# B's diagonal images by DMA, dt matmuls in pairs on two row tiles, and a new job order for a scan kernel on four engines

## The reference

```
xi, z = split(h_normed @ in_proj);  xi = silu(causal_conv4(xi))
dt, Bm, Cm = split(xi @ x_proj)                 # 16, 16, 16 columns
dt  = softplus(dt @ dt_proj + dt_bias)          # 512 channels
dA  = exp(dt[..., None] * A);  dBu = dt[..., None] * Bm * xi[..., None]
h_t = dA_t * h_(t-1) + dBu_t                    # scan over time, 512 channels x 16 states
y   = sum_s(h * Cm) + xi * D;  out = (y * silu(z)) @ out_proj;  h += out
```

## Time and profile before

| | |
|---|---|
| time, median of 3 runs | 8187.27 us (8179.34 to 8187.66) |
| time of the profiled execution | 8192.45 us |
| its span, first to last instruction | 8190.5 us |
| PE busy | 7500.0 us (92%) |
| PEld busy | 5200.0 us (63%) |
| DVE busy | 6520.6 us (80%) |
| ACT busy | 5866.5 us (72%) |
| POOL busy | 6376.4 us (78%) |
| mean granted clock of TensorE | 0.978 of full |

### The profile page before, as it was taken

How to read it: one execution, slowest core, us unless ns; L and a number is a source line. 1 busy time by engine, 2 the same in 40 slices (tenths; PEclk the granted TensorE clock), 3 DMA queues, 4 the chain that set the end, 5 groups by cost and what they waited for, 6 DMA issues and landing times. The chain is left out here.

```text
span 8190.5 us, 204523 instructions
## 1 busy us (share of the span) xinstructions
PE 7500.0 (92%) x86656; PEld 5200.0 (63%) x86656; DVE 6520.6 (80%) x6490; ACT 5866.5 (72%) x10937; POOL 6376.4 (78%) x3556
## 2 busy tenths in 40 slices
PE   7888799999989899999988899999988899999989
PEld 4666466666664566666664666666664666666655
DVE  4888799999984499999983599999973699999972
ACT  5776687878774578787764678877764687778753
POOL 5886399999991499999980599999980699999970
PEclk8998899999999999999999999999999999999999
DMA  1111111111110111111110111111110111111110
GB/s 60 52 53 60 43 52 50 64 46 50 46 48 27 43 63 49 50 46 50 52 42 27 58 50 46 50 46 60 56 38 21 54 50 46 50 59 57 46 39 11
DMA packets 133325, 391.29 MB, mean 48 GB/s; under 512 B 49580, under 2 KB 78188, under 8 KB 95552
## 3 DMA queue, kind: packets, MB, share of 16 engines
q1 hardware_dynamic: 132416, 378.22, 13.1%
HBM read 364.93 MB, written 13.24 MB: 46 GB/s over the span
## 5 line engine op out<-in xcount | busy, mean ns | idle before, releaser
L1220 DVE TENSOR_TENSOR_SCAN arena<-arena,ps 128x512 f32<-128x512 f32 x4608 | 5341.5, 1205 | 606.1 <-issue 380.3
L1445 POOL TENSOR_TENSOR arena<-arena 128x1024 f32<-128x1024 f32 x2240 | 5250.6, 2365 | 428.7 <-DVE arena L1220 399.6
L563 PEld LDWEIGHTS ps<-arena 64*128 64x128 f32 x36864 | 2334.3, 190 | 1338.3 <-issue 750.5
L897 ACT ACTIVATE arena<-arena,rate 128x511 f32<-128x511 f32 (+1 forms) x4608 | 3036.3, 710 | 43.3 <-DVE arena L1220 43.0
L563 PE MATMUL ps<-arena 64*128 64x128 f32 x36864 | 2759.6, 286 | 266.9 <-DVE arena L1220 260.9
L582 PE MATMUL ps<-csts,arena 64*128 64x64 f32 x35840 | 1516.1, 223 | 27.8 <-POOL arena L1445 27.8
L582 PEld LDWEIGHTS ps<-csts,arena 64*128 64x128 f32 x35840 | 1432.3, 140 | 40.7 <-POOL arena L1445 33.7
L621 PE MATMUL ps<-arena 128*128 128x512 f32 x1152 | 633.3, 650 | 144.8 <-DVE arena L1250 137.8
L1454 POOL TENSOR_TENSOR arena<-csts,arena 128x512 f32<-128x512 f32 x576 | 603.1, 1049 | 81.1 <-ACT arena L1022 81.1
L894 ACT ACTIVATE arena<-arena 128x2 f32<-128x2 f32 x2048 | 405.4, 198 | 326.7 <-DVE arena L1220 319.5
L661 PE MATMUL ps<-arena 128*128 128x512 f32 x1120 | 604.1, 636 | 15.6 <-DVE arena L1255 7.7
(11 more groups left out here) (118 smaller groups left out, 7014.6 us busy)
## 6 DMA issues: line engine op xcount, KB each, us to landing
arena<-c_rows SPq DMA_DIRECT2D x288, 1024.0 KB, 4.8
arena<-ip_x SPq DMA_DIRECT2D x20, 512.0 KB, 4.4
arena<-ip_z SPq DMA_DIRECT2D x20, 512.0 KB, 4.1
arena<-op_w SPq DMA_DIRECT2D x20, 512.0 KB, 3.8
hT<-xT SPq DMA_DIRECT2D x16, 512.0 KB, 3.7
arena<-w SPq DMA_DIRECT2D x8, 1024.0 KB, 5.2
out<-arena SPq DMA_DIRECT2D x64, 128.0 KB, 1.7
arena<-xp_w SPq DMA_DIRECT2D x20, 160.0 KB, 2.5
```

Source lines behind the costliest of these rows:

```text
L563: i = nc.tensor.matmul(o, dtxT[half[h], c, b, :], diagB[half[h], pair, b, :].rearrange("p (i s) -> p i s", s=Q), start=True, stop=True)
L897: nc.scalar.activation(o, i, ACT.Exp, scale=rate[:, ph.layer(n), g:g + 1]).then_inc(decay.sem, 1)
L1220: nc.vector.tensor_tensor_scan(hs[:, place(n, v) + g % 2, :], dA[:, g % RING, :], pair[:, g % Q::Q], 1.0 if ph.main() else 0.0, ALU.mult, ...
L1445: nc.gpsimd.tensor_tensor(hs[:, a:a + 2, :], hs[:, a:a + 2, :], Crep[:, 2 * pair:2 * pair + 2, :], ALU.mult).then_inc(prod.sem, 1)
```

## The change

1. POOL's `diag` is gone. SP keeps two images of the full `diagB` layout in DRAM (`b_image`, 2 MB each, zeroed once at the start). In each step it writes B's values onto the diagonals with two DMAs of 64 partitions (each 2,048 runs of 8 bytes), waits until they have landed, and then loads the eight parts of `diagB` (256 KB each, in runs of 512 bytes), each when PE has made the last input that reads the old part. PE waits on these loads (`diag_loaded`). The order of B's and C's loads on SP is written out in `LOADS`.
2. `xp` gives 97 rows: dt and the one stand a second time behind B, in rows 80 to 96. `dt0` and `dt2` multiply rows 0 to 32, `dt1` and `dt3` rows 64 to 96 (B's rows there meet zeros in the weights), in two banks, next to each other in PE's table. `bT` transposes only rows 64 to 96.
3. `rstd` no longer loads its table in main steps from the third of a block on.
4. The tables of PE, ACT, DVE and POOL and the banks are new, for main and prefix steps. SP's `body` is split into `fetch`, `replace` and `after`; in main steps the load of `op_w` comes after the loads of B and C.

```diff
-XP = 80
+XP = 97
+DT_ROWS = DR + DS + 1
...
-MAIN_PE = {0: [("z1.1", 1)], 2: [("z2.0", 1), ("z2.1", 1)], 3: [("z3.0", 1)], 4: [("z3.1", 1)], 5: [("yt2", -1)],
-           6: [("yt3", -1), ("xp.0", 1)], 7: [("xp.1", 1), ("xp.2", 1)], 8: [("xp.3", 1), ("dxT3", 0)], 9: [("bT", 1)],
-           10: [("dt2", 1)], 11: [("dt3", 1), ("ms", 2)], 12: [("dt0", 1)], 13: [("dt1", 1)],
-           15: [("out0.0", -1), ("out0.1", -1)], 16: [("out0.2", -1)], 17: [("out0.3", -1)], 18: [("xi0.0", 2)],
-           19: [("xi0.1", 2), ("yt0", 0)], 20: [("dxT0", 1)], 21: [("xi1.0", 2)], 22: [("xi1.1", 2)], 23: [("yt1", 0)],
-           24: [("xi2.0", 2)], 25: [("xi2.1", 2), ("dxT1", 1)], 26: [("out1.0", -1)],
+MAIN_PE = {0: [("z1.1", 1), ("z2.0", 1)], 2: [("z3.0", 1), ("z2.1", 1)], 3: [("z3.1", 1)], 5: [("yt2", -1)],
+           6: [("xp.0", 1), ("xp.1", 1), ("yt3", -1)], 7: [("xp.2", 1), ("xp.3", 1)], 8: [("dxT3", 0)], 9: [("bT", 1)],
+           10: [("dt2", 1), ("dt3", 1)], 12: [("dt0", 1), ("dt1", 1)], 14: [("ms", 2)],
+           15: [("out0.0", -1), ("out0.1", -1), ("out0.2", -1)], 16: [("out0.3", -1)], 18: [("xi0.0", 2)],
+           19: [("xi0.1", 2), ("yt0", 0)], 20: [("dxT0", 1)], 21: [("xi1.0", 2), ("xi1.1", 2)], 22: [("yt1", 0)],
+           24: [("xi2.0", 2), ("xi2.1", 2)], 25: [("dxT1", 1)], 26: [("out1.0", -1)],
...
-            12: [("dt0", 1), ("skip3", 0)], 13: [("dt1", 1), ("rstd", 2)], 14: [("soft", 1), ("carry", 1)], 19: [("xi0", 2)],
+            12: [("dt0", 1), ("dt1", 1), ("skip3", 0)], 13: [("rstd", 2)], 14: [("soft", 1), ("carry", 1)],
...
-PRE_ACT_FIRST = {2: [("yev3", -1)], 10: [("yev0", 0)], 19: [("yev1", 0)], 28: [("yev2", 0)]}
+PRE_ACT_FIRST = {3: [("yev3", -1)], 10: [("yev0", 0)], 19: [("yev1", 0)], 26: [("yev2", 0)]}
...
+LOADS = [("B", 0), ("B", 1), ("B", 2), ("B", 3), ("C", 0), ("B", 4), ("B", 5), ("C", 1), ("B", 6), ("B", 7), ("C", 2),
+         ("C", 3)]
...
-                    pe.wait_ge(diag_ready.sem, diag_ready.at(ph, n, pair + 1))
+                    pe.wait_ge(diag_loaded[pair], ph.count(1, n, 1) * 16)
...
-                    i = nc.tensor.matmul(o, dtw[0:DR + DS + 1, c * P:(c + 1) * P], xdbl[0:DR + DS + 1, :],
-                                         start=True, stop=True)
+                    rows = slice(B_ROW, XP) if c % 2 else slice(0, DT_ROWS)
+                    i = nc.tensor.matmul(o, dtw[rows, c * P:(c + 1) * P], xdbl[rows, :], start=True, stop=True)
...
-                    nc.scalar.preload_act_table_set(LOG_EXP)
+                    if not ph.main() or m < 2:
+                        nc.scalar.preload_act_table_set(LOG_EXP)
...
-            def diag(ph, m, pair):
...
+                    for h in range(2):
+                        sp.dma_start(diagonal(m % 2, h), xbc[half[h], m % 2, :, :].rearrange("p b (q s) -> p (b q) s", s=Q)
+                                     ).then_inc(b_stored, 16)
+
+            def replace(ph, n):
+                m = n + 1
+                if m < ph.steps:
+                    sp.wait_ge(b_stored, ph.count(1, m, 1) * 32)
+                    sp.sem_inc(passed, 1)
+                    for what, k in LOADS:
+                        if what == "B":
+                            sp.wait_ge(input_ready.sem, input_ready.at(ph, n, PAIRS - CQ + k + 1))
+                            sp.dma_start(diagB[:, k, :, :], image(m % 2)[k]).then_inc(diag_loaded[k], 16)
+                        else:
+                            sp.wait_ge(prod.sem, prod.at(ph, n, UNITS - CU + 2 * k + 2))
+                            sp.dma_start(Crep[:, 4 * k:4 * k + 4, :],
+                                         c_rows[m % 2, 4 * k:4 * k + 4, :].partition_broadcast(P)).then_inc(c_loaded[k], 16)
```

More of the change, by code:

```diff
@@ L27 @@
 NB = T // P
+IMAGE = P * NB * CQ * P
 RING = 8
@@ L43 @@
 PRE_BANK = {"out0": 1, "yt3": 0, "out1": 0, "dxT1": 0, "ms": 1, "dxT2": 0, "xi0": 0, "xi1": 1, "dxT3": 0, "xi2": 0,
[L44 to L47, removed]
+            "xi3": 1, "z0": 0, "z1": 0, "z2": 1, "z3": 1, "yt0": 0, "xp": 1, "yt1": 1, "bT": 1, "dt2": 1, "dt3": 0,
@@ L48 @@
+            "dt0": 1, "dt1": 1, "yt2": 1, "dxT0": 0}
+MAIN_BANK = {"z0": 0, "z1": 1, "z2": 0, "z3": 1, "yt2": 0, "yt3": 1, "xp": 0, "dxT3": 1, "bT": 1, "ms": 1, "dt0": 0,
+             "dt1": 1, "dt2": 0, "dt3": 1, "out0": 0, "xi0": 1, "yt0": 0, "dxT0": 0, "xi1": 1, "yt1": 0, "xi2": 1,
              "dxT1": 0, "out1": 0, "xi3": 1, "dxT2": 1}
 PARTS = {"ms": KD, "xi": KD, "z": KD, "xp": KI, "out": KI}
-PRE_PE = {1: [("dxT1", 0), ("out0.1", -1)], 2: [("out0.2", -1)], 3: [("yt3", -1)], 5: [("out0.3", -1), ("out1.0", -1)],
[5 rows of a table removed]
@@ L203, in program @@
 def program(nc, xT, ctxT, w_early, ip_x, ip_z, xp_w, dt_w, op_w, a_log, d_par, pre_w1, pre_w2, cst,
-            cst_attention, avec, wq, wk, wv, wp, w1, w2, b2, kept, c_rows, out):
+            cst_attention, avec, wq, wk, wv, wp, w1, w2, b2, kept, c_rows, b_image, out):
     ctx = ExitStack()
@@ L634, in job @@
                     await_read_of(pe, ph, m, "xp")
+                    rows = slice(B_ROW, XP)
                     for b in range(NB):
-                        i = nc.tensor.matmul(o[:, b * XP:(b + 1) * XP], xdbl[0:XP, b::NB], eye[0:XP, 0:XP],
+                        i = nc.tensor.matmul(o[:, b * DT_ROWS:(b + 1) * DT_ROWS], xdbl[rows, b::NB], eye[rows, rows],
                                              start=b == 0, stop=b == NB - 1, is_transpose=True)
@@ L1486, in body @@
                         event(ph, m, name)
-                    if v >= UNITS - CU and ph.has(n, 1):
-                        diag(ph, n + 1, v - (UNITS - CU))
             def attend(ph, then):
@@ L1518, in rows, with image, diagonal @@
                 return v.rearrange("(k p) m -> p k m", p=P)
+            def image(par):
+                return b_image[par * IMAGE:(par + 1) * IMAGE].rearrange("(p b q c) -> q p b c", p=P, b=NB, q=CQ)
+            def diagonal(par, h):
+                row = IMAGE // P
+                a = par * IMAGE + h * 64 * row
+                rows_of = b_image[a:a + 64 * (row + Q)].rearrange("(i x) -> i x", i=64)
+                return rows_of[:, 0:row].rearrange("i (g c) -> i g c", c=P)[:, :, 0:Q]
             for dst, src in ((csts[:, :], cst), (avecs[:, :], avec), (rate[:, :, :], a_log), (Dall[:, :, :], d_par)):
@@ L1522, in _, with next_out, fetch @@
             sp.wait_ge(cst_ready, 1)
+            def next_out(ph, n):
+                if 1 <= n < ph.steps and ph.slot(n - 1) == ph.slots - 1:
+                    await_done(sp, ph, n - 1, "out1")
+                    sp.dma_start(opw, rows(op_w[ph.layer(n)])).then_inc(opw_loaded, 16)
             def body(ph, n):
+                fetch(ph, n)
+                if n + 1 >= 0:
+                    replace(ph, n)
+                    after(ph, n)
+            def fetch(ph, n):
                 m = n + 1
@@ L1548, in body @@
                                  ).then_inc(init_loaded, 16)
-                if 1 <= n < ph.steps and ph.slot(n - 1) == last:
-                    await_done(sp, ph, n - 1, "out1")
-                    sp.dma_start(opw, rows(op_w[ph.layer(n)])).then_inc(opw_loaded, 16)
+                if not ph.main():
+                    next_out(ph, n)
                 if m < ph.steps:
@@ L1570, in body, with after @@
                     sp.sem_inc(passed, 1)
-                    for k in range(4):
-                        sp.wait_ge(prod.sem, prod.at(ph, n, UNITS - CU + 2 * k + 2))
-                        sp.dma_start(Crep[:, 4 * k:4 * k + 4, :], c_rows[m % 2, 4 * k:4 * k + 4, :].partition_broadcast(P)
-                                     ).then_inc(c_loaded[k], 16)
+                    if ph.main() or m > 1:
+                        for k in range(CQ):
+                            sp.wait_ge(diag_loaded[k], ph.count(1, m, -1) * 16)
+                        sp.sem_inc(passed, 1)
+                    elif m == 0:
+                        sp.wait_ge(image_ready, 32)
+                        sp.sem_inc(passed, 1)
+                    await_read_of(sp, ph, m, "bT")
+                    for h in range(2):
[5 more added lines that the diff above has]
+                    sp.wait_ge(b_stored, ph.count(1, m, 1) * 32)
+                    sp.sem_inc(passed, 1)
+                    for what, k in LOADS:
[6 more added lines that the diff above has]
+                                         c_rows[m % 2, 4 * k:4 * k + 4, :].partition_broadcast(P)).then_inc(c_loaded[k], 16)
+            def after(ph, n):
+                m = n + 1
+                if ph.main():
+                    next_out(ph, n)
                 if ph.main() and m == ph.steps:
@@ L1589, in body @@
                     sp.wait_ge(kept_state.sem, kept_state.at(ph, n, UNITS))
-                    half = ph.slot(n) * SEGS
-                    sp.dma_start(kept[ph.layer(n), half:half + SEGS, :, :].rearrange("b p w -> p b w"),
+                    at_row = ph.slot(n) * SEGS
```

(11 more changed lines are left out.)

55 lines of the change are left out of this document (28 added, 27 removed), and 36 rows, old and new, of tables (MAIN_ACT, MAIN_DVE, PRE_ACT, PRE_DVE).

## The result

The changed kernel takes 7796.59 us (median of 4 runs, 7792.45 to 7799.68) against 8187.47 us: a ratio of 0.952, with a 95% interval of 0.951 to 0.954. The forecast was 7975 us, the range 7850 to 8140. The direction was right; the gain of 391 us is nearly twice the 212 us that the steps of the prediction add up to.

What follows compares the result with a forecast made beforehand. PE and DVE, coupled, were taken to bound a main step, with POOL off its path. 64 main steps at 2.4 us (154) plus the prefix (58) made 212 us, giving 7975 us; range 7850 to 8140 (its own 7870 to 8050).

Steps and rivals of the forecast that it cites:

- the images are hidden: Stores and loads of B's images by DMA: cost 0 in both kinds of step, up to 4.5 us per prefix step.
- The waits on `yev2`: Prefix step: PE's wait of 6.09 us for ACT's `yev2` behind `soft` goes, as `yev2` now stands ahead of it.
- 1.3 + 1.1 us: Main step: 1.3 from the earlier scan that waits for ACT, 1.1 from later slots; 2.4 us less, 92.0 us.
- the scan that waits for ACT: Main step: DVE's scan that stood 1.76 us for its exponentials behind `rstd`, `soft`, `carry`; forecast to come 1.3 us earlier.
- Later slots: Main step: second halves of `xi1`, `xi2` one slot earlier; half of PE's 1.37 + 0.75 us waits, 1.1 (bounds 0 and 2.1).
- The pairs: The four dt matmuls run as two pairs on different row halves: 1.6 us of PE saved (bounds 0 and 2.0).
- `rstd` and `ms`: Main step: dropped table load saves ACT 1.28 us, `ms` moves up to 2.95 us later; net, the scan comes 1.3 earlier.
- PE's floor: Main step: PE's remaining busy time as lower limit of the step, 89.58 - 1.9 = 87.7 us.
- The prefix: Prefix step: 6.1 + 2.6 + 1.6 - 1.2 = 9 us less; 58 us over all prefix steps.
- The 2.6 us for the clock: Prefix step: granted clock 0.95 read as 5.3 us at half speed, costing 2.6 us; most of it goes.
- POOL's term: Prefix step: POOL's 93.96 us of work would have come within 3 us of the new length; without `diag` it doesn't.
- The 1.6 us for dt: Prefix step: the saving by paired dt matmuls, counted there too at 1.6 us.

Runs made afterwards that it cites:

- images_only: The kernel before with only B's images by DMA instead of POOL's `diag` (`xp`, `bT` and SP's order as changed): 8134.78 us, against 8187.47 before.
- diag_on_pool: The changed kernel with POOL's eight `diag` back and no image of B: 7866.74 us, against 7796.59 for the changed kernel.
- split_xi: The changed kernel with the second halves of `xi1` and `xi2` one slot later again in PE's main table: 7896.31 us, against 7796.59.
- split_groups: The changed kernel with the parts of `z`, `xp`, `out0`, `xi1` and `xi2` back at their old slots in PE's main table: 7955.89 us, against 7796.59.
- ms_13: The changed kernel with `ms` of the main step on PE at slot 13 instead of 14: 7754.55 us, against 7796.59.
- yev2_late: The changed kernel with `yev2` of the prefix step back at slot 28, behind `soft`: 7829.35 us, against 7796.59.
- no_pairs: The changed kernel with `dt1` and `dt3` on rows 0 to 32 too, so no two dt matmuls run together: 7869.33 us, against 7796.59.
- gate2_late: The changed kernel with DVE's `gate2` of the main step back from place 11 to 13: 7858.57 us, against 7796.59.
- old_others: The changed kernel with all main-step tables but PE's (ACT, DVE, POOL) as before the change: 7921.51 us, against 7796.59.

## Why the prediction was wrong

*What sets the pace was right, the size was wrong.* PE and DVE set a main step, POOL did not, and the images are hidden: images_only and diag_on_pool show the last two. The waits on `yev2` and its slow clock went as forecast. But the sum for a main step, 1.3 + 1.1 us, was short in both of its terms: up to the scan that waits for ACT the step lost 2.1 us, behind it 2.5.

*The step that failed: "Later slots".* It priced only the second halves of `xi1` and `xi2`, at 1.1 us out of two rows of PE's waits. split_xi measures 1.66: of its two rows the 0.75 us stayed, while the 1.37 us went with the tap's wait behind it, and 0.3 us of PE's work came on top. The halves of `z`, `xp` and `out0` that moved beside others were priced at nothing; split_groups less split_xi gives 1.06 us. Together 2.7 us of a main step instead of 1.1. The change was read as moves in time, and not as which matmul comes next to which.

*The pairs.* 1.6 us of PE forecast; undoing them alone gives 0.77 us of PE's busy time and 0.97 us of the step. The prediction took off 0.4 us for the overlap with inputs that was there already, and the trace has more of it.

*`rstd` and `ms`.* Forecast was a scan that comes 1.3 us earlier; counted from chunk 0's first sum it came 2.1 earlier, but not by this sum. The dropped load, put at 1.28 us, was worth 0, the pairs were worth half, and the move of `ms`, put at up to 2.95 us of ACT's chain, costs 1.0 us of a step: ms_13 gets that back. `xp` and `gate2`, which also stand in this stretch, had no term.

*PE's floor.* Forecast 87.7 us, measured 86.54. Of the 3.04 us less, undoing single parts tells 1.04 for the five groups and 0.77 for the pairs, and images_only, where little but `bT` differs on PE, gives 0.47. The other 0.8 us are not told apart.

*The prefix.* 9 us forecast, 12.3 measured. `yev2` was sized at 6.1 + 2.6 - 1.2 = 7.5 us; undone alone it measures 4.8 in the step shown, since where it goes PE waits for POOL and scans instead. The 2.6 us for the clock rest on a slip: a mean of 0.95 over 106 us, at levels of 1 and one half, is a tenth of the time at the lower level, 10.6 us, not 5.3. That 2.6 is near the 1.79 us of PE's work which yev2_late adds is luck: some 4 of its 10 us at the lower level fall into the wait itself (clock 0.66 over 375.70 to 381.80), where PE has nothing to do. POOL's term was taken as cover alone ("would have come within 3 us of the new length"); with the new order it is worth 8 us, since POOL's `dtx` and products stand behind `diag`s just where PE then waits. So the step that failed in the prefix is this term, put at nothing. The 1.6 us for dt were worth nothing there (no_pairs), and of the other places of the prefix order, which had no price, only their sum of 4.5 us beside the images is known.

*What stays open.* The single terms don't add: undoing them one at a time costs 2.7 + 0.97 + 1.92 us of a main step, and the images gave 0.6 to the old order, 6.2 in all against the 5.0 that it lost. gate2_late shows one way in which that comes about: a wait that only the new order of PE brings out. How the remainder of old_others divides over ACT's, DVE's and POOL's places is not known.

## What to carry to other kernels

In a table of jobs on PE, look not only at when each job comes but at what it stands between: a job of another row count among small matmuls pays a price each time it stands alone, until the group is so long that the engine coupled to PE runs dry. A wait between two coupled engines has a cause one step further back; ask for the wait of the instruction that ended it before it is priced. And an engine that is nearly full and off the path can be a second wait behind the first: in the prefix step the images alone gave 3.0 us, the new order alone 4.4, both 12.3; in the main step POOL at 99% held up nothing.

## What was not expected of the hardware

- Two matmuls of 128 x 512 between units of 64-row matmuls take 1.06 us from start to next start, four 1.91, six 2.77: some 0.2 us for each change of the kind of matmul and back.
- 4,096 runs of 8 bytes from SBUF to DRAM took 0.008 us of a DMA engine each, and landed 5.4 us after issue, where the prediction's bounds, from the nearest row before, allowed for 5.3 to 26 us of transfer alone.
